# VectorE takes the up product of one token chunk straight from the bank, and two layer norms start later

## What is computed

```
x = x + attention0(norm(x)) + ffn0(norm(x))    # attention0: linear, elu + 1 features; ffn0: ternary weights
x = x + attention1(norm(x)) + ffn1(norm(x))    # attention1: rotary, softmax; ffn1: Hadamard transforms in the weights
ffn0: hidden = silu(xn Wu) * (xn Wg);                    out = hidden Wd
ffn1: hidden = silu(xn Wg * wsg) * (xn Wu * wsu);        out = hidden Wd'
```

## Time and profile before

| | before |
|---|---|
| median of three runs | 733.77 us (733.51 to 735.02) |
| the profiled execution: its time | 733.87 us |
| the profiled execution: span, first to last instruction | 731.9 us |
| mean granted TensorE clock, share of full speed | 0.988 |

### The profile page before, as it was taken

How to read it: one execution, slowest core, us unless ns; L and a number is a source line. 1 busy time by engine, 2 the same in 40 slices (tenths; PEclk the granted TensorE clock), 3 DMA queues, 4 the chain that set the end, 5 groups by cost and what they waited for, 6 DMA issues and landing times.

```text
span 731.9 us, 11063 instructions
## 1 busy us (share of the span) xinstructions
PE 699.4 (96%) x4246; PEld 441.6 (60%) x4246; DVE 523.9 (72%) x856; ACT 438.4 (60%) x600; POOL 299.1 (41%) x269
## 2 busy tenths in 40 slices
PE   7787999989999899999999999999999999999998
PEld 6576888977777688677676773333333333333445
DVE  7888865654667467678778788988896388888315
ACT  3463435346555432432432338999998899999883
POOL 2247844348577842542543431122233223332410
PEclk9999999989999999999999999999999999999999
DMA  7255001011025642413110012345444244423321
GB/s 269 75 214 180 1 12 47 1 58 58 1 87 172 226 148 87 143 61 114 59 59 25 34 63 73 120 140 166 123 141 139 90 146 146 145 93 91 111 75 58
DMA packets 25848, 74.14 MB, mean 101 GB/s; under 512 B 4620, under 2 KB 5996, under 8 KB 24964
## 3 DMA queue, kind: packets, MB, share of 16 engines
q1 hardware_dynamic: 21268, 65.37, 26.7%
q0 software_dynamic: 3808, 7.60, 3.5%
q10 hardware_dynamic: 720, 0.48, 0.2%
HBM read 54.54 MB, written 23.06 MB: 106 GB/s over the span
## 4 chain that ended last, share of the span: by engine, by line
PE 62%; POOL 2%; DVE 2%; ACT 1%; issue 1%; DMA 1%; SPq 0%; DVEq 0%; POOLq 0%; ACTq 0%
PE PS L1038 17%; PE PS L769 12%; PE PS L1024 12%; PE PS L775 9%; PE PS L1007 6%; PE PS L997 5%; DVE mx L1338 1%; POOL sg L1651 1%; DMA scr_k<-spl 1%; POOL rot L1671 1%; POOL rot L1672 1%; PE PS L1013 0%; ACT P L1550 0%; ACT spl L1532 0%; ACT us L1515 0%
## 5 line engine op out<-in xcount | busy, mean ns | idle before, releaser
L1550 ACT ACTIVATE P<-PS 128x1024 f32<-128x1024 f32 x256 | 249.1, 1024 | 30.0 <-PE PS L1024 29.7
L1345 DVE TENSOR_REDUCE mx<-PS 128x1 f32<-128x512 f32 x300 | 189.1, 682 | 32.2 <-PE PS L1007 30.6
L1338 DVE TENSOR_REDUCE mx<-PS 128x2 f32<-128x1024 f32 x106 | 124.8, 1221 | 37.3 <-PE PS L997 37.0
L1038 PE MATMUL PS<-P,VV 128*32 128x512 f32 x1024 | 136.5, 605 | 0.1
L1642 POOL TENSOR_TENSOR hl<-sg,hh 128x512 fp32r<-128x512 f32 x64 | 85.2, 1331 | 117.6 <-ACT hh L1520 67.4
L1024 PEld LDWEIGHTS PS<-QS,KS 64*128 64x128 f32 x512 | 48.5, 183 | 121.3 <-ACT P L1550 109.4
L1024 PE MATMUL PS<-QS,KS 64*128 64x512 f32 x512 | 116.5, 456 | 0.9 <-DVE mx L1338 0.6
L1007 PE MATMUL PS<-KM,QM 64*128 64x512 f32 x300 | 81.1, 396 | 0.0
L1506 ACT ACTIVATE sg<-PS,cols 128x512 f32<-128x512 f32 x32 | 22.0, 688 | 82.3 <-PE PS L769 82.3
L1651 POOL TENSOR_TENSOR sg<-sg,us 128x512 f32<-128x512 f32 x32 | 42.0, 1313 | 37.5 <-ACT us L1515 37.5
L769 PE MATMUL PS<-XH,UGH 128*128 128x512 f32 x128 | 54.1, 423 | 1.6 <-ACT sg L1506 0.8
(11 more groups left out here) (211 smaller groups left out, 1361.3 us busy)
## 6 DMA issues: line engine op xcount, KB each, us to landing
QM<-scr_q SPq DMA_DIRECT2D x16, 512.0 KB, 4.4
KM<-scr_k SPq DMA_DIRECT2D x16, 512.0 KB, 5.3
QS<-scr_q SPq DMA_DIRECT2D x16, 512.0 KB, 4.3
KS<-scr_k SPq DMA_DIRECT2D x16, 512.0 KB, 5.3
scr_q<-spl SPq DMA_DIRECT2D x24, 256.0 KB, 3.3
scr_k<-spl SPq DMA_DIRECT2D x24, 256.0 KB, 3.4
scr_o<-OE POOLq DMA_DIRECT2D x14, 256.0 KB, 2.7
stg<-in_tern SPq DMA_DIRECT2D x3, 1024.0 KB, 4.8
```

Of the source, the lines that this page charges most:

```text
L1038: i = e.matmul(PS[32 * c:32 * c + 32, 7, :], v_head(8 * b + kt, 2 * j + c // 2), P[s % 4][:, chunk(c // 2 + 2 * (c % 2))], start=(kt == 0) ...
L1338: e.tensor_reduce(mx[p % 2][:, :, qt, half], PS[:, b:b + 2, :], AX.X, ALU.max).then_inc(q["mx"], 2)
L1345: e.tensor_reduce(mx[p % 2][:, h, qt, half:half + 1], bank[b], AX.X, ALU.max).then_inc(q["mx"], 1)
L1550: e.activation(P[s % 4][:, half * 1024:(half + 1) * 1024], PS[:, b:b + 2, :].rearrange("p b n -> p (b n)"), ACT.Exp).then_inc(q["ex"], 1)
```

## The change

Two edits. `NORMS` starts the norm of chunk 0 at (0, 2, 14) in place of (0, 2, 2), that of chunk 1 at (0, 2, 22) in place of (0, 2, 10), and that of chunk 2 at (0, 3, 10) in place of (0, 3, 8). And in the first chunk of layer 1 (steps 32 to 39) VectorE computes (bank * wsu) * sg in one instruction from the bank, as in layer 0; ScalarE's copy us and GpSimd's product are gone there, and the up bank is freed by VectorE's product. Chunks 1 to 3 of layer 1 are as before.

```diff
--- before.py
+++ after.py
@@ -265,7 +265,7 @@
         put("load_m", 1)
 
 
-    NORMS = {(0, 2, 2): 0, (0, 2, 10): 1, (0, 3, 8): 2, (1, 0, 5): 3}
+    NORMS = {(0, 2, 14): 0, (0, 2, 22): 1, (0, 3, 10): 2, (1, 0, 5): 3}
 
     def main(layer):
         norm, again = iter(()), False
@@ -960,7 +960,7 @@
                     sums(bank[b], wide(TG, None, m * 128, c)).then_inc(q["u"], 1)
                 else:
                     sums(bank[b], wide(UGH, UGL, m * 128, c)[3:], start=False).then_inc(q["u"], 1)
-                freed[b] = (q["h"], f + 1) if layer == 0 else (q["ue"], f - 31)
+                freed[b] = (q["h"], f + 1) if layer == 0 or c == 0 else (q["ue"], f - 39)
 
             def ffn_end(layer, c):
                 for k in range(2):
@@ -1267,13 +1267,17 @@
                     e.scalar_tensor_tensor(s[:, :], s[:, :], 1.0, bank[b], ALU.add, ALU.mult).then_inc(q["v1"], 1)
 
             def up(layer, c, m, b):
+
+                f = 32 * layer + 8 * c + m
+                s = sg[f % 3]
+                if layer and c:
+                    return
+                e.wait_ge(q["u"], f + 1)
+                e.wait_ge(*(q["v1"], f + 1) if layer == 0 and c < WHOLE else (q["t"], f + 1))
                 if layer:
-                    return
-                f = 8 * c + m
-                s = sg[f % 3]
-                e.wait_ge(q["u"], f + 1)
-                e.wait_ge(*(q["v1"], f + 1) if c < WHOLE else (q["t"], f + 1))
-                e.tensor_tensor(s[:, :], s[:, :], bank[b], ALU.mult).then_inc(q["h"], 1)
+                    e.scalar_tensor_tensor(s[:, :], bank[b], col("wsu", m), s[:, :], ALU.mult, ALU.mult).then_inc(q["h"], 1)
+                else:
+                    e.tensor_tensor(s[:, :], s[:, :], bank[b], ALU.mult).then_inc(q["h"], 1)
 
             def ffn_end(layer, c):
                 e.wait_ge(q["d"], 32 * layer + 8 * (c + 1))
@@ -1510,7 +1514,7 @@
                 if layer == 0:
                     e.wait_ge(q["h"], f + 1)
                     e.activation(hh[f % 4][:, :], sg[f % 3][:, :], ACT.Copy).then_inc(q["hh"], 1)
-                else:
+                elif c:
                     e.wait_ge(q["u"], f + 1)
                     e.activation(us[f % 4][:, :], bank[b], ACT.Copy, scale=col("wsu", m)).then_inc(q["ue"], 1)
 
@@ -1645,9 +1649,9 @@
                 f = 32 * layer + 8 * c + m
                 if layer == 0:
                     low_part(f)
-                else:
+                elif c:
                     s = sg[f % 3]
-                    e.wait_ge(q["ue"], f - 31)
+                    e.wait_ge(q["ue"], f - 39)
                     e.tensor_tensor(s[:, :], s[:, :], us[f % 4][:, :], ALU.mult).then_inc(q["h"], 1)
 
             def hidden(c, m):
```

## The result

The change took 737.33 us in the median of 10 runs (734.83 to 740.0) against 733.71 us of the kernel before (10 runs, 732.65 to 737.25): a ratio of 1.0039 with a 95% interval from 1.0023 to 1.0055. It is slower; the forecast was 729.3 us and its range ended at 732.9. The profiled execution took 736.81 us (span 734.9).

What follows compares the result with a forecast made beforehand. TensorE, 96% busy, was taken to set the pace, losing time to waits and clock falls. Terms -6.6 + 2.7 + 2.4 + 0.8 - 0.6 - 3.3 = -4.6 us took 733.87 to 729.3 us, range 725.2 to 732.9.

Steps and rivals of the forecast that it cites:

- Term 1: End of the first attention: norm 0 leaves it, removing waits, lost clock and eight transposes, -6.6 us.
- Terms 2 and 3: Weight preparation in layer 0: the norm now inside it adds waits, +2.7 us, and the clock falls there, +2.4 us.
- Term 4: Chunk 3 of layer 0: norm 1's transposes move in, +0.8 us; the rest of norm 1 lies beside TensorE's work.
- Term 5: Norm 2 two places later in layer 0: a 2.1 us wait for rotations replaces 2.7 us of costs, -0.6 us.
- the clock falls a second time in layer 0: Rival: the clock also falls in the 2.1 us wait at norm 2's transposes, 2.4 us more, 731.7 us; chance 0.22.
- Term 6: Layer 1, steps 32 to 39: VectorE's product removes VV waits and the clock's fall, adds one 2.0 us wait, -3.3 us.
- VectorE the bound: Rival: in layer 1's first chunk VectorE's product is late every step, 5.9 us instead of -3.3, 738.5 us; chance 0.10.
- The two places of low clock: Where TensorE was taken to be idle or slow: first attention's end, 152 to 160 us, and layer 1's first chunk, 254 to 259.

Runs made afterwards that it cites:

- e6: The change with norm 0 started four positions earlier, at (0, 2, 10), ahead of ScalarE's weight copies: 732.28 us, ratio 0.9981.
- e9: The change with the applications of norms 0 and 1 moved from ScalarE to VectorE: 729.72 us, ratio 0.9934.
- e8: The change with the four applications of norm 1 moved from ScalarE to VectorE, at the same places of the order: 733.5 us, ratio 0.9994.
- e2: The kernel before with only the new NORMS, layer 1's product as before: 740.81 us, ratio 1.0088.
- e7: e5 with norm 2 started two positions later, at (0, 3, 10), as in the change: 728.2 us, ratio 0.9924.
- e10: e9 with step 33 by the old route (ScalarE's copy, GpSimd's product): 727.79 us, ratio 0.9921.
- e3: The change with norm 1's second half put directly behind its first half in chunk 3 of layer 0: 736.99 us, ratio 1.0044.
- e1: The change with the old order of the norms, so only VectorE's product in layer 1's first chunk: 731.74 us, ratio 0.9971.
- e11: e5 with norms 0 and 1 applied by VectorE in place of ScalarE: 726.48 us, ratio 0.9897.
- e4: e1 with step 33 by the old route (ScalarE's copy, GpSimd's product): 729.85 us, ratio 0.9948.
- e5: e4 with the third side bank joining once the second key-value sum is over, not after the attention: 728.56 us, ratio 0.9925.

## Why the prediction was wrong, point by point

- **Term 1** (-6.6, measured -7.0): right. No wait stands before either `att_b`.
- **Terms 2 and 3** (+5.1 together, measured +4.8): right in place and releaser, and the sum closer than its parts. Waits of 2.1 and 1.9 us were worked out, 2.02 and 1.35 came, the first transposes 10.4 us after T as forecast; so the waits cost 2.1 us more than before and not 2.7, and the clock, at 0.50 for 6 us in which TensorE was busy for 4.64, some 2.7 with its edge and not 2.4. e6 and e9 show both terms to be avoidable.
- **Term 4** (+0.8, measured +6.1) is **the step that failed**: "The rest of norm 1 lies beside TensorE's work, which had no wait between 181 and 204 us." I walked ScalarE's and VectorE's queues for norm 0 in the preparation and did not for norm 1 in chunk 3, and put the absence of waits in the place of slack. The ring of hh, UGH, UGL and product had none. Of the 5.3 us that were missed, 2.56 are the two waits; the clock at 0.59 in 4.0 us costs 1.6 (4.0 x 0.41); 1.1 is not in any wait of 0.3 us or more. e8 takes 3.3 of them back by moving 2.2 us off ScalarE, 1.1 in the two waits and most of the rest in the clock, and with them the loss: 0.9994 [0.998, 1.0008], which can't be told from before. COS, the other thing that the term left open, was not late: its load began at 193.86 us and took 3.7 us to land, and VectorE's first rotation, at 202.32 us, waited for TensorE.
- **Term 5** (-0.6, measured -0.35): the size was right in this execution. The wait is 2.66 us, ended by a rotation, not 2.1. But the clock did fall behind the same wait in the profiles of e2, e7, e8, e9 and e10, as the rival "the clock falls a second time in layer 0" has it; it held in those of the change, e3 and e6. That one and the same program does either I take to be so, but no run here shows one program both ways. If the change's other executions fell there as those five, that would account for some of the 2.6 us between its cuts and its median; no run here shows the clock by place in more than one execution of it, so that stays open.
- **Term 6** (-3.3, measured -2.6): right in mechanism. No wait for VV and no fall of the clock in layer 1; one new wait for the product of 1.75 us (2.0 forecast), ended by VectorE. A second of 0.32 us that I had not seen makes up half of the difference. e1 alone confirms it: -2.6 us in the runs.
- **VectorE the bound** (738.5 us, 0.10) gave nearly the measured time for the wrong reason. VectorE's product holds TensorE in two of eight steps. The Trainium skill (Perfetto Trace Analysis, Identifying the Most-Contended Engine) says to optimize the engine of highest occupancy first; that the work should therefore not go to VectorE, the busiest engine behind TensorE, was my reading of it. The runs bear it out in part only: e1, e8, e9 and e11 gave VectorE more work and were faster than their counterparts with less, while e4 and e10 took one product off it, that of step 33, and were faster by 1.9 us each. What decided was who waited at that place, not the share of the whole span.
- **The range** ended at 732.9. Term 4, alone of the six besides the well-measured term 1, had no bounds, and a missing bound is read as zero; at +6.1 in its place the sum of the same terms gives 734.6 us.
- **The two places of low clock** that the prediction starts from are not all: the trace of before has two more, with windows at 0.50, at 32 to 38 and at 64 to 68 us. The change touches neither, and no term goes by them, but they too differ from one execution to the next.

## What to carry to other kernels

An engine that never waits proves that its suppliers keep up, not that they have time over: before work is moved beside it, follow one round of the suppliers through every engine that hands on to another, and compare its length with the step that it feeds. Two engines that are each idle for a third of a step can be a closed ring without slack. An addition that falls where the other engine waits for it then comes out whole, with the clock's fall on top (2.8 us of norm and of waiting for it on ScalarE made two rounds 2.7 us longer); one on the engine that is idle at that moment mostly does not (1.67 us on VectorE in e8 made them 0.38 us longer), so that is where to put it. And when a step is worth 2 us by its waits, walk the queues at the place it goes to with the same care as at the place it leaves.

## What the runs showed of the hardware

- **The length of one wait doesn't settle whether the clock falls.** The 2.66 us wait before norm 2's transposes was followed by a fall of the clock in five kernels' profiles (0.50 to 0.57 in the lowest window of 2 us) and by 1.00 in three; in e5 two waits of 0.64 and 0.62 us with transposes between were enough for 0.57 over 3.5 us, while 0.84 and 0.46 us in the same place of e11, and 1.51 and 0.41 us in chunk 3 of e9, left it at 1.00.
- **The start-up varies by itself.** The clock at 12 to 18 us was 1.00 in one profiled execution and 0.50 in another of the same program text up to there, and the same `att_n` group came at 118.15 us in the one and at 120.00 in the other; over all fourteen profiles it came at 118.15 to 122.58 us. Two single executions of this kernel can't be compared closer than that unless both are cut at a common instruction.
- **The same norm is cheaper on VectorE.** Its piece of 128x256 takes 0.40 us there in the median (0.62 at most, in e8) and 0.59 on ScalarE, and needs no nmr first.
